# First attention of a two-layer block on one core: turned probabilities in two PSUM banks, values of four units in one run, relative values by halves, one key side, sums transposed

## What is computed

```python
dist = jnp.clip(idx[None, :] - idx[:, None], -R, R) + R          # R = 64
pe_k = rel_emb_k[dist]
pe_v = rel_emb_v[dist]
...
q = q / jnp.sqrt(jnp.asarray(hd, x.dtype))
score = jnp.einsum('bhqd,bhkd->bhqk', q, k) + jnp.einsum('bhqd,qkd->bhqk', q, pe_k)
attn = jax.nn.softmax(score, axis=-1)
ctx = jnp.einsum('bhqk,bhkd->bhqd', attn, v) + jnp.einsum('bhqk,qkd->bhqd', attn, pe_v)
ctx = jnp.transpose(ctx, (0, 2, 1, 3)).reshape(b, s, d)
return ctx @ W_out + b_out
```

## Time and profile before

| what | us |
|---|---|
| median of the runs | 2518.97 (3 runs, 2514.1 to 2520.15) |
| span of the profiled execution | 2521.2 |
| busy over the span: PE / DVE / ACT / POOL | 2267.4 / 1915.6 / 1737.9 / 841.7 |
| loop of the first attention, 256 steps | about 445 to 1558 |
| first four sequences of the second attention, 32 steps | about 1558 to 1664 |

### The profile page before, as it was taken

One profiled execution on the slowest core, in us unless ns is written; L12 is line 12 of the kernel. 1 busy time (PEld: TensorE's weight loads), 2 busy tenths in 40 slices (PEclk: granted clock), 3 DMA queues, 4 the chain that ended last, 5 costly groups with the idle time before them and its releaser, 6 DMA issues. The chain is left out here.

```text
span 2521.2 us, 90789 instructions
## 1 busy us (share of the span) xinstructions
PE 2267.4 (90%) x34592; PEld 1784.8 (71%) x34592; DVE 1915.6 (76%) x7571; ACT 1737.9 (69%) x5614; POOL 841.7 (33%) x911
## 2 busy tenths in 40 slices
PE   6999998799889899888989989879999699999998
PEld 5888887577777777777777777557878466666665
DVE  6777773567777777777777777658888588888888
ACT  2333332677777777777777777866666599999988
POOL 3666665021111111111111212221121556556452
PEclk9999998899999999999999999989999799999999
DMA  7857442666666666666667764023322111111110
GB/s 242 237 157 193 115 111 51 162 162 162 168 171 171 171 168 171 165 168 168 164 165 175 170 166 116 14 72 111 106 98 78 38 35 35 31 37 34 30 36 14
DMA packets 360773, 304.79 MB, mean 121 GB/s; under 512 B 25368, under 2 KB 328856, under 8 KB 358952
## 3 DMA queue, kind: packets, MB, share of 16 engines
q1 hardware_dynamic: 349864, 271.93, 42.5%
q0 software_dynamic: 10496, 27.28, 3.6%
HBM read 166.43 MB, written 132.69 MB: 119 GB/s over the span
## 5 line engine op out<-in xcount | busy, mean ns | idle before, releaser
L823 ACT ACTIVATE probs<-neg_scores,low 128x256 f32<-128x256 f32 (+1 forms) x1152 | 574.2, 500 | 240.3 <-DVE low L959 226.4
L959 DVE CUSTOM_DVE_ANT_0 neg_scores<-scores,rel_bias 128x256 f32<-128x256 f32 x1024 | 373.6, 421 | 248.3 <-PE scores L1122 118.2
L1136 PE MATMUL probsT<-consts,probs 128*128 128x128 f32 x2240 | 360.6, 284 | 52.7 <-ACT probsT_s L839 48.2
L1136 PEld LDWEIGHTS probsT<-consts,probs 128*128 128x128 f32 x2240 | 248.1, 142 | 108.5 <-ACT probsT_s L839 68.5
L774 POOL TENSOR_SCALAR q_heads<-q_raw,consts,q_bias 128x256 f32<-128x256 f32 x128 | 69.2, 553 | 749.1 <-ACT q_raw L805 749.0
L1686 DVE CUSTOM_DVE_ANT_0 neg_scores<-scores,alibi 128x128 f32<-128x128 f32 (+1 forms) x896 | 266.1, 353 | 62.4 <-PE scores L1742 58.6
L275 POOL TENSOR_TENSOR hid<-hid,gate_bc 128x512 f32<-128x512 f32 x160 | 205.5, 1289 | 152.3 <-DVE hid L448 141.9
L301 ACT ACTIVATE ga<-gate_up 128x512 f32<-128x512 f32 x160 | 95.6, 597 | 224.4 <-PE gate_up L514 214.1
L967 DVE COPY rel_s<-scores 128x768 f32<-128x768 f32 x256 | 243.9, 953 | 4.4 <-PE scores L1122 3.1
L1648 ACT ACTIVATE probs<-neg_scores,low 128x128 f32<-128x128 f32 (+1 forms) x448 | 199.5, 447 | 55.6 <-DVE low L1686 46.6
L1112 PE MATMUL scores<-k_sides,q_heads 32*128 32x256 f32 (+1 forms) x2304 | 206.1, 424 | 25.7 <-DVE rel_s L967 20.0
(11 more groups left out here) (205 smaller groups left out, 4977.9 us busy)
## 6 DMA issues: line engine op xcount, KB each, us to landing
rel_rows<-rel_s SPq DMA_DIRECT2D x256, 192.0 KB
rel_bias<-rel_rows SPq DMA_DIRECT2D x256, 192.0 KB, 3.4
gate_bc<-gate_rows SPq DMA_DIRECT2D x32, 1024.0 KB, 10.2
rel_rows<-rel_s SPq DMA_DIRECT2D x256, 128.0 KB
rel_bias<-rel_rows SPq DMA_DIRECT2D x256, 128.0 KB, 3.1
packed<-ffn_in SPq DMA_DIRECT2D x8, 1280.0 KB, 15.1
xe<-packed SPq DMA_DIRECT2D x16, 640.0 KB, 3.9
expert_out<-ye POOLq DMA_DIRECT2D x16, 640.0 KB, 3.2
```

The costliest lines, as they stand in the source:

```text
L823: act.activation(probs[s % 3][:, j, 0:w], neg[s % 2][:, j, 0:w], ACT.Exp, bias=low[s % 3][:, j:j + 1], scale=-1.0, accum_out=sums[s // UB ...
L959: dve.tensor_tensor_reduce(neg[s % 2][:, j, 0:w], S_ps[:, 512 * j:512 * j + w], bias_of(s)[:, j, :] if s < NU0 else alibi[:, 4 * j + s % 4 ...
L1136: ins = pe.transpose(PT_ps[:, j * P:(j + 1) * P], probs[u % 3][:, j, kt * P:(kt + 1) * P], ident)
```

## The change

- The two halves of the turned probabilities get a bank each (`PT_ps` becomes a list of two), and PE turns both halves of a unit in one run at the start of a step. The second bank was that of the relative values.
- Values are no longer made unit by unit: `values(g)` makes those of four units (one query tile, 32 matmuls) every fourth step, into one half of `O_ps`.
- Relative values go into the other half of that bank, in two runs of 32 matmuls (`relative_values`, half 0 and 1) in two further steps. `z` is filled in two operations of 256 columns instead of one of 512, and `ctx_s` in two of 128 columns instead of one of 256.
- `turn_a` and `turn_b` become one run of 64 matmuls, `turn_relative`, at r = 5, and the job `context` at r = 6, in which the inverse sums are transposed with `transpose` instead of multiplied by the identity.
- PE does its job between the turns and the scores of a step, and ACT and DVE move it in the same step (`jobs_at.get(s, ())`) instead of the next.
- The keys get one side, without the far bias (which is constant over the keys).

```diff
-            PT_ps = bank_m("probsT0")
+            PT_ps = [bank_m(f"probsT0_{kt}") for kt in range(KT)]
             O_ps = bank_m("values0")
-            RV_ps = bank_m("relative_values0")
...
-                            for i in range(2):
-                                ins = act.activation(k_of[b % 2][:, i, :], M_ps[:, 0:S], ACT.Identity, bias=key_bias[:, i:i + 1])
+                            ins = act.activation(k_of[b % 2][:, :], M_ps[:, 0:S], ACT.Identity, bias=wview["bk"])
...
-                    for name, b in jobs_at.get(s - 1, ()):
+                    for name, b in jobs_at.get(s, ()):
                         move(name, b)
...
-                    if s >= 9 and s % 4 == 1 and s // 4 - 2 < 2 * nb:
...
+                    g = (s - 7) // 4
+                    if s >= 7 and s % 4 == 3 and g < 2 * NB0:
+                        dve.wait_ge(valued, g + 1)
...
+                        dve.tensor_copy(ctx_s[:, g % 2 * P:(g % 2 + 1) * P], O_ps[:, 0:P]).then_inc(ctx_moved, 1)
+                    for half in range(2):
+                        g = (s - 8 - half) // 4
+                        if s >= 8 and s % 4 == half and 0 <= g < 2 * nb:
+                            dve.wait_ge(rel_valued, 2 * g + half + 1)
...
-                    for name, b in jobs_at.get(s - 1, ()):
+                    for name, b in jobs_at.get(s, ()):
                         if name == "v":
...
+                    if name == "context":
+                        pe.wait_ge(inverted, b + 1)
+                        for qt in range(2):
+                            ins = pe.transpose(M_ps[:, S + qt * P:S + (qt + 1) * P], rinv_c[:, qt, :, :].rearrange("p h c -> p (h c)"), ident)
...
                 for s in STEPS:
                     if 0 <= s - 2 < NUL:
-                        turn(s - 2, 0)
-                    if 0 <= s - 3 < NUL:
-                        value(s - 3)
-                    if 0 <= s - 6 < NU0:
-                        relative_value((s - 6) // 4, (s - 6) % 4)
-                    if 0 <= s - 2 < NUL and width(s - 2) == S:
-                        turn(s - 2, 1)
+                        turn(s - 2)
+                    for name, b in jobs_at.get(s, ()):
+                        project(name, b)
...
-                    for name, b in jobs_at.get(s, ()):
-                        project(name, b)
+                    g, r = divmod(s - 6, 4)
+                    if r == 0 and 0 <= g < 2 * NB0:
+                        values(g)
+                    if r in (1, 2) and 0 <= g < 2 * nb:
+                        relative_values(g, r - 1)
+                    if r == 3 and g % 2 == 1 and 0 <= g < 2 * nb:
+                        turn_relative(g // 2)
```

More of the change, by code:

```diff
@@ L684, in program @@
                     job_list.append((s, "prefix", (b - 4) // 2))
-                if r == 5 and 1 <= b <= nb:
-                    job_list.append((s, "turn_a", b - 1))
                 if r == 6 and 1 <= b <= NB0:
-                    job_list.append((s, "turn_b", b - 1))
+                    job_list.append((s, "context", b - 1))
             job_no = {}
             for _, name, b in job_list:
-                job_no[name, b] = 1 + sum(1 for other, _ in job_no if other != "turn_a")
+                job_no[name, b] = 1 + len(job_no)
             jobs_at = {}
@@ L1099, in project, with turn_relative @@
                                 ins = pe.matmul(o, earlier, chosen[:, i, :], start=(i == 0), stop=True)
-                    if name != "turn_a":
-                        ins.then_inc(spare_full, 1)
+                    ins.then_inc(spare_full, 1)
+                def turn_relative(b):
+                    pe.wait_ge(spare_free, job_no["context", b] - 1)
+                    pe.wait_ge(rel_masked, 4 * b + 4)
+                    where = z[:, :, :].rearrange("p t (g h q) -> p t g h q", g=8, q=4)
+                    for t in range(4):
+                        for i in range(4):
+                            for j in range(4):
+                                rows = slice(32 * j, 32 * j + 32)
+                                at = (t * 4 + i) * 32
+                                pe.matmul(M_ps[rows, 0:S].rearrange("p (t g q) -> p t g q", t=2, g=8)[:, :, :, 4 * t:4 * t + 4],
+                                          cview["pick_head"][:, at:at + 32], where[:, :, :, 4 * i + j, :],
+                                          start=(i == 0), stop=(i == 3), skip_group_check=True)
                 def score(u):
@@ L1112, in score @@
                         ins = pe.matmul(S_ps[:, 512 * j:512 * j + w], q_of[b % 2][rows, i, qt * P:(qt + 1) * P],
-                                        k_of[b % 2][rows, qt if b < nb else 0, 0:w], start=True, stop=True)
+                                        k_of[b % 2][rows, 0:w], start=True, stop=True)
                     return ins
@@ L1158, in relative_value, with turn @@
-                def relative_value(g, part):
-                    qt = g % 2
-                    if part == 0:
-                        pe.wait_ge(moved1, 4 * g + 4)
-                        if g >= 1:
-                            pe.wait_ge(rel_masked, g)
-                    for G in (2 * part, 2 * part + 1):
+                def turn(u):
+                    pe.wait_ge(exped, 4 * (u + 1))
+                    for kt in range(width(u) // P):
+                        if kt == 0 and u >= 1:
+                            pe.wait_ge(moved0, u)
+                        if kt == 1 and second_halves(u):
+                            pe.wait_ge(moved1, second_halves(u))
+                        for j in range(4):
+                            ins = pe.transpose(PT_ps[kt][:, j * P:(j + 1) * P], probs[u % 3][:, j, kt * P:(kt + 1) * P], ident)
+                        ins.then_inc(turned, 1)
@@ new lines, in values @@
+                def values(g):
+                    b, qt = g // 2, g % 2
+                    pe.wait_ge(moved0, 4 * g + 4)
+                    pe.wait_ge(moved1, second_halves(4 * g + 4))
+                    if qt == 0:
+                        pe.wait_ge(spare_free, job_no["v", b])
+                    if g >= 1:
+                        pe.wait_ge(ctx_moved, g)
+                        pe.wait_ge(rel_masked, 2 * min(g, 2 * nb))
+                    halves = width(4 * g) // P
+                    for i in range(4):
+                        for kt in range(halves):
+                            for j in range(4):
+                                rows = slice(32 * j, 32 * j + 32)
+                                ins = pe.matmul(O_ps[rows, 0:P], v_of[b % 2][:, kt, i, rows], probsT[:, qt, i, kt, j, :],
+                                                start=(i == 0 and kt == 0), stop=(i == 3 and kt == halves - 1), skip_group_check=True)
+                    ins.then_inc(valued, 1)
@@ L1165, in relative_value, with relative_values @@
+                def relative_values(g, half):
+                    qt = g % 2
+                    if half == 0:
+                        pe.wait_ge(ctx_moved, g + 1)
+                    else:
+                        pe.wait_ge(rel_masked, 2 * g + 1)
+                    for G in range(4 * half, 4 * half + 4):
                         for kt in range(KT):
```

95 lines of the change are left out of this document (22 added, 73 removed).

## The result

| what | before | after |
|---|---|---|
| median of the runs, us | 2516.53 (4 runs, 2509.3 to 2520.2) | 2549.09 (4 runs, 2548.3 to 2554.5) |
| span of the profiled execution | 2521.2 | 2546.9 |
| loop of the first attention, 256 steps | 1112.9 | 1147.4 |
| second attention in the same loop, start of the first to start of the last of 32 steps | 98.4 | 95.2 |
| 16 steps, mean of 13 such blocks | 70.03 | 72.19 |

The changed kernel is slower: ratio 1.0132, 95% interval 1.0111 to 1.0152. The forecast was 2517 us and its range ended at 2534, so the time lies outside it. All of the loss is in the loop of the first attention. The later stages are 8 us shorter.

The account below looks back on a forecast made before the run. Bounds were taken as PE's scores and the band's return from HBM, about equal, with DVE's work third. Sixteen steps at 69.8 us gave +2 us in the loop, the second attention -4: 2517 us, range 2495 to 2534.

Parts of the forecast that it names:

- PE's work: PE in the first attention's loop: fewer changes of tile shape and cheaper inverse sums save 2.0 us of work per sequence.
- The rule of four bounds: Loop step length: larger of PE's path, DVE's path and 3.5 us for minima-to-scores; band's way round makes two steps 8.3 us.
- Both heavy steps: DVE at even r = 7 (slot chain meets softmax) and odd r = 6 (context before norm's end): 5.9 and 5.1 us.
- the walk's 69.8 us: Sixteen loop steps after the change, each starting by the previous step's length or two steps before plus 8.3 us.
- PE would wait for DVE before the scores: Sign of being right, in the loop: PE's waits for ACT go and waits for DVE replace them; no size given.
- The band's way round: Relative scores through HBM, from the end of `rel_s` to minima two steps later: 6.0 us, plus 2.3, 8.3 for two steps.
- That DVE's idle time would move to the band: Sign of being right: DVE's idle time before minima moves from waiting for PE's scores to waiting for the band.
- full waits for jobs: End of the forecast where DVE waits fully for same-step jobs: 70.6 us for 16 steps, +14 us in the loop.
- The second attention: Its 32 steps, without a band, lose PE's waits for the turned bank and key move: 4 us saved, between 0 and 9.
- The loss rival: DVE's full waits for jobs or a slower band lose 14 to 18 us in the loop: 2535 us, chance 0.20.
- The third rival, PE alone: DVE's chains hidden, PE alone sets the loop's pace: 66.6 us for 16 steps, 2463 us in all, chance 0.03.
- the three signs: Wrong if steps after light ones average under 4.0 us, DVE shows no job waits, or ACT's copies hold up DVE's minima.

Follow-up runs that it names:

- The run with no falls: The changed kernel with 148 needless matmuls on PE in sixteen steps, where it waits longest for DVE: 2540.9 us, 1.0089 of the kernel before.
- e9_norm_earlier: The changed kernel with only the layer norm one step earlier, slot chain left in place: 2695.9 us, 0.9827 of the kernel before, slower kind of chip.
- e2_even_dve: The changed kernel with DVE's slot chain two steps earlier, layer norm's start and end one earlier, slot weights at odd r = 0: 2516.6 us, 0.9994 of before.
- e4_jobs_as_before: The changed kernel with jobs put back at the end of PE's step and moved one step later: 2510.4 us, 0.9972 of the kernel before.
- paced: POOL's router scatters sent out one per step; on the kernel before: 2514.4 us on the first kind of chip, 2676.5 on the slower kind.
- e8_before_split: The kernel before with DVE's two longest chains (router choice, slots) cut in two: 2722.6 us, 0.9942 of the kernel before, slower kind of chip.

## Why the prediction was wrong

- **PE's work: right in direction, a little less than forecast.** The values of four units took 2.02 us with the last matmul (1.96 to the next start), the relative values 1.03, the 64 matmuls of `turn_relative` 1.92; 1.76 and 1.8 were put down with the changes of shape beside them. The waits for ACT are gone. PE's busy time fell by 1.5 us per sequence, for 2.0.
- **The rule of four bounds: right in its pattern, short in its sum.** Walked with 8.3 us for two steps, the prediction's list gives 4.0, 4.3, 4.0, 4.3, 4.7, 3.6, 4.7, 5.9 for the even sequence and 3.5, 4.8, 3.5, 4.8, 3.5, 4.8, 5.1, 4.3 for the odd one. Measured were 4.6, 4.0, 3.9, 4.6, 4.9, 3.7, 5.2, 6.0 and 3.7, 4.9, 4.1, 5.3, 3.8, 4.5, 5.3, 3.8. Both heavy steps, put down as 5.9 and 5.1, came as 6.0 and 5.3. But the sum is 72.2 for 69.8.
- **The step that failed: the walk's 69.8 us, which stood level with the kernel before.** It was 2.4 us too short in 16 steps, 38 us in the loop, while the same walk of the kernel before was short by 0.3. Two terms of it can be named, the granted clock and the band.
- **The granted clock had no term.** The earlier trace rows had it at 1.00, and the prediction took that for granted. It forecast that PE would wait for DVE before the scores, as a sign only, without asking how long one such wait is. A step where DVE takes 4.8 to 6 us and PE has 2.4 to 3 us of work leaves PE idle in one piece. Eighteen times the clock fell behind such a piece. The run with no falls shows that this cost at least 8 us. By the correlation, 1.1 to 1.9 us each, 17 falls more than before would make 19 to 32 of the 34.5 us lost in the loop; e9_norm_earlier, with nine falls more and less time, speaks against the upper part of that.
- **The band's way round was taken too short.** In the rows above `rel_s` ended at 1111.63 (1110.68 and 0.95) and the minima two steps later began at 1117.76, after a wait for the band: 6.1 us, for 6.0 taken. But that is one place. Over 206 steps of the loop the minima waited for the band 34 times, with a mean of 6.25 us, and 54 times with 6.38 in the kernel before. The 6.0 had been chosen because it reproduced the kernel before. An estimate by the same walk with 6.3, 8.6 us for two steps: 70.8 before and 71.6 after, 13 us longer in the loop instead of 2. The measured 71.45 without falls lies near that. With the moved chains in the steps where two of the runs have them (e2_even_dve: 5.0 at even r = 5, 4.3 at r = 7, 4.1 at odd r = 6; e4_jobs_as_before: 5.0 at even r = 5, 4.3 at r = 7, 4.8 at odd r = 0, 4.1 at odd r = 6, and 3.5 for the v job's step) the walk gives 69.9 and 70.0, and 70.45 and 69.9 were measured. The kernel before speaks against it (70.8 by the walk, 70.0 measured). That DVE's idle time would move to the band was wrong: its waits for it fell from 66.6 to 34.1 us, and those for PE's scores rose from 83.6 to 89.2.
- **The remainder is open.** Even r = 6 and odd r = 2 and 3 hold most of the shortfall. In even r = 6 DVE waited 1.4 us in the mean for the context job (1.1 without falls), where the prediction put no wait, and at most 0.7 elsewhere; odd r = 2 and 3 were 0.8 us shorter without falls. The end "full waits for jobs" was given as 70.6, and even without falls 71.45 was measured. How the loss divides between clock, band and waits for jobs no run shows. What e2_even_dve and e4_jobs_as_before do show is that it hangs on DVE's chains and on the jobs being moved in the same step: either edit removes all of it.
- **The second attention: right.** 3.2 us less, for 4.
- **The rivals.** The loss rival had the right sign and the right engine, DVE with its same-step moves, but 2535 as its price; e4_jobs_as_before shows that this one edit costs 39 us. The third rival, PE alone, had 2463: PE's busy time per step did fall (3.94 to 3.76 us), but the path did not follow it. By the start times of the earlier trace rows a change of tile shape takes 0.11 to 0.18 us; no run here takes these changes away by themselves.
- **What would show it wrong.** None of the three signs came: the steps after light ones took 4.6 us in the mean and not under 4.0, DVE did wait for jobs, and its minima waited for ACT only 6.5 us between 600 and 1500 us. The signs were all of the terms in the sum, none of the term that was missing, and none was for a band slower than taken.

## What to carry to other kernels

When a change takes work off a PE that waits for another engine in some steps, list PE's idle time as single pieces, not as a total: every fall of the clock in the changed kernel's loop stood behind a piece of 1.7 us or more, and evening out DVE's steps gave back all of the time that was lost, with no less work on any engine. Moving a job's hand-over into the same step saves no work and couples two engines more closely; here it cost 39 us with two banks and 111 with one, and should be tried alone. A bound that is chosen because it reproduces the kernel before should be measured as well, since the new kernel may lean on it more. And bunched indirect transfers are worth spreading, which gave 65 us on one kind of chip and 4 on the other, and a comparison within 2% should be repeated on another chip, because both kernels may differ in something that only one chip makes visible.

## What the runs showed of the hardware

- The sign of this change depends on the chip: 1.0132 on the first, 0.9849 (0.9819 to 0.9879) on another. The kernel before loses about 65 us there to one collision in 16 steps, which one number removes (2742 to 2676). The changed kernel shows little of it (its step odd r = 3 is 5.5 us there and 5.3 on the first kind), but it was not run paced there.
- On that kind of chip PE stood still for up to 1.4 us at a time (1.43 in e8_before_split) amid a run of matmuls of 32 columns while POOL issued five indirect transfers back to back (0.3 us apart). On the first kind the same issues, as far apart, did not hold PE up in the kernel before: its step odd r = 3 is 4.6 us long and has no such gap. What PE waits for then is open: the trace names no releaser.
- The stages behind the loop took 980 us instead of 860 on that kind, with every kernel; from 1700 to 2500 us the granted clock was 0.92 to 0.94 there and 0.96 to 0.99 on the first kind. That was not followed up.
